# First heads' stacks and negated queries made under the second batch's projections; the opening without 42 unread matmuls

## The reference, cut to what matters

```
x = x + LN(attn(LN(x)))         # 16 heads of 16, rotary q and k, softmax over all 2048 keys, all f32
    q, k = rope(x Wq' + bq), rope(x Wk' + bk);  v = x Wv' + bv
    out  = softmax(q k' / 4) v;  return out Wo' + bo
x = x + LN(ffn(LN(x)))          # 2 layers: windowed attention with 8 heads of 64, then a gated MLP
```

## Time and profile before

| | |
|---|---|
| median of 3 runs | 2952.65 us (2952.53, 2952.65, 2959.49) |
| the profiled execution | 2961.71 us, its span 2959.7 us |
| PE busy in the span | 2797.1 us (95%) |
| DVE, ACT, POOL busy | 2320.3 us, 2116.6 us, 972.5 us |
| mean granted clock of PE | 0.965 of full speed |
| projections / first gap / opening | 0 to 123 us / 123 to 161 us / 147 to 198 us |

### The profile page before, as it was taken

The page is one execution under the profiler, slowest core; times in us unless marked ns, Lnnn a source line. Parts: engine busy times, 40 slices in busy tenths (PEclk is TensorE's granted clock), DMA queues, the critical chain, the costliest instruction groups (busy, mean ns, idle before and its releaser), DMA issues. The chain is left out here.

```text
span 2959.7 us, 59044 instructions
## 1 busy us (share of the span) xinstructions
PE 2797.1 (95%) x22548; PEld 1742.8 (59%) x22548; DVE 2320.3 (78%) x4282; ACT 2116.6 (72%) x4556; POOL 972.5 (33%) x1145
## 2 busy tenths in 40 slices
PE   7689999999999999999976799999999999999997
PEld 7543333333333333333335688888888788888886
DVE  6559999999999999899905577777777677777774
ACT  5458888888888888788854466666666666667664
POOL 6510000010001000000007455555555465665563
PEclk9859999999999999899988799999999999999999
DMA  5612333334343343334212000000000100000000
GB/s 161 173 27 31 59 54 56 53 66 73 61 71 58 62 72 59 57 50 71 41 53 102 3 5 4 5 5 4 5 5 32 54 11 19 19 11 19 19 18 25
DMA packets 84328, 131.32 MB, mean 44 GB/s; under 512 B 32912, under 2 KB 58960, under 8 KB 76240
## 3 DMA queue, kind: packets, MB, share of 16 engines
q1 hardware_dynamic: 77760, 120.41, 20.9%
q10 hardware_dynamic: 6288, 7.14, 0.7%
HBM read 83.98 MB, written 34.60 MB: 40 GB/s over the span
## 5 line engine op out<-in xcount | busy, mean ns | idle before, releaser
L634 ACT ACTIVATE probs<-scores 128x512 f32<-128x512 f32 x2048 | 1114.9, 596 | 203.2 <-PE scores L565 80.8
L667 DVE TENSOR_REDUCE mx<-aux 128x1 f32<-128x1024 f32 x982 | 1201.1, 1223 | 65.7 <-PE aux L533 58.5
L533 PE MATMUL aux<-k_stack,q_stack 48*128 48x512 f32 x2006 | 760.8, 455 | 15.5 <-DVE mx L675 10.5
L565 PE MATMUL scores<-q_stack,k_stack 50*128 50x512 f32 x2048 | 764.6, 452 | 0.0
L578 PE MATMUL pv<-probs,v_ones 128*32 128x256 f32 x8192 | 661.0, 395 | 0.1
L565 PEld LDWEIGHTS scores<-q_stack,k_stack 50*128 50x128 f32 x2048 | 311.1, 186 | 431.1 <-ACT probs L634 413.6
L578 PEld LDWEIGHTS pv<-probs,v_ones 128*32 128x32 f32 x8192 | 161.9, 108 | 362.7 <-ACT probs L634 291.0
L533 PEld LDWEIGHTS aux<-k_stack,q_stack 48*128 48x128 f32 x2006 | 307.9, 189 | 47.0 <-DVE mx L675 21.0
L484 POOL CAST m_parts<-head_max 128x16 fp32r<-128x16 f32 x32 | 6.3, 198 | 933.7 <-DVE head_max L660 933.7
L1399 ACT ACTIVATE VO<-VO,wo_bo_sb 128x256 f32<-128x256 f32 (+1 forms) x512 | 250.9, 491 | 47.3 <-DVE wo_bo_sb L1523 47.0
L1523 DVE CUSTOM_DVE_ANT_0 VO<-bank,mask_sb,wo_bo_sb 128x256 f32<-128x256 f32 (+1 forms) x512 | 216.2, 469 | 56.2 <-PE bank L1229 56.2
(11 more groups left out here) (172 smaller groups left out, 4706.5 us busy)
## 6 DMA issues: line engine op xcount, KB each, us to landing
q_stack<-qk_dram SPq DMA_DIRECT2D x192, 128.0 KB, 5.3
k_stack<-qk_dram SPq DMA_DIRECT2D x192, 128.0 KB, 7.0
qk_dram<-qkT_hi SPq DMA_DIRECT2D x32, 256.0 KB, 3.1
qk_dram<-qkT_lo SPq DMA_DIRECT2D x32, 256.0 KB, 3.6
VO<-o_stage SPq DMA_DIRECT2D x128, 32.0 KB, 7.0
q_minus_first<-sums_dram SPq DMA_DIRECT2D x32, 128.0 KB, 3.0
w_parts<-tables SPq DMA_DIRECT2D x16, 256.0 KB, 2.5
x_in<-x_dram SPq DMA_DIRECT2D x16, 256.0 KB, 3.2
```

Source lines behind the costliest of these rows:

```text
L533: return nc.tensor.matmul(out, q_stack[max_rows, n % BODY, tile * P:(tile + 1) * P], k_stack[max_rows, n % BODY, keys * 512:(keys + 1) * 512],
L565: last = nc.tensor.matmul(out, k_stack[0:SCORE_ROWS, n % BODY, s * P:(s + 1) * P], q_stack[0:SCORE_ROWS, n % BODY, j * 512:(j + 1) * 512], ...
L634: nc.scalar.activation(probs[:, e % PROBS], scores[:, item_of_exp(e) % BANKS1], ACT.Exp, scale=float(D1) ** -0.5).then_inc(act_emptied, 1)
L667: nc.vector.tensor_reduce(mx[:, n % BODY, tile, half:half + 1], aux[:, unit % 2].rearrange("p a k -> p (a k)"), AX.X, ALU.max).then_inc(dv ...
```

## The change

- `q_stack`, `k_stack` and `q_minus_first` belong to a class `Stacks` that is allocated before the projections. The rows of -1 are set by POOL at the beginning of the projection phase.
- In the projection phase SP loads head 0's twelve DMAs behind the stores of group 4 and head 1's twelve behind the stores of group 5. POOL negates in five pieces (4 tiles each of head 0, and 5 of head 1), after its steps 26, 28, 30, 32 and 33.
- SP no longer waits at the end of the projection phase for the stores; it does in the attention phase, before it loads the rows with the maxima of head 0.
- The L593 matmuls (two a tile, 42) are left out.
- Space is made elsewhere: `qk_rot` is written over `qk_cos` (so L143 waits for the transposes of tile `t - 2` instead of for its rotation), the raw weights lie in `VO`, the opening's positive parts in four slots of `probs`, `x1_sb` is a ring of 16 tiles (POOL's L779 waits from the ninth pair on for the store and the reader 16 tiles back), several tiles of the feed-forward phase lie in the stacks, and `b2` is loaded through a DRAM copy.

```diff
+Q_MINUS_PIECES = ((0, 0, 4), (0, 4, 8), (0, 8, 12), (0, 12, TB), (1, 0, LEAD))
@@ project_phase, SP @@
                         sp.dma_start(rows[:, tokens], tile[:, g % 2, c].bitcast(F32)).then_inc(stored[g % 2], 16)
-            for g in range(2):
-                sp.wait_ge(stored[g], 16 * STORES * (NT // GROUP // 2))
+                if g == TB // GROUP:
+                    for parity in range(2):
+                        sp.wait_ge(stored[parity], 16 * STORES * (TB // GROUP // 2))
+                if g in (TB // GROUP, TB // GROUP + 1):
+                    n = g - TB // GROUP
+                    sp.wait_ge(stacks.minus_ones_made, n + 1)
+                    stacks.load(sp, n, 0, stacks.for_scores_loaded)
+                    stacks.load(sp, n, SECOND, stacks.for_max_loaded)
@@ project_phase, DVE @@
-                        dve.wait_ge(rot_done, t - 1)
+                        dve.wait_ge(qkT_in_psum, t - 1)
@@ project_phase, POOL @@
+            for n in range(BODY):
+                nc.gpsimd.memset(stacks.k[SECOND // 2:SECOND, n].bitcast(F32), -1.0).then_inc(stacks.minus_ones_made, 1)
...
+                if t in NEGATED_AT:
+                    negate(NEGATED_AT.index(t))
@@ attention_phase, SP @@
-                if i == 0:
-                    sp.wait_ge(dve_emptied, unit_of[(OPENING - 1) * BLOCKS] + 1)
...
-            load(0, SECOND, for_max_loaded)
-            for n in range(2):
-                sp.wait_ge(minus_ones_made, n + 1)
-                load(n, 0, for_scores_loaded)
-                if n == 0:
-                    load(1, SECOND, for_max_loaded)
+            for parity in range(2):
+                sp.wait_ge(qkT_stored[parity], 16 * STORES * (NT // GROUP // 2))
             load_rows(0)
@@ attention_phase, POOL @@
-            for n in range(BODY):
-                nc.gpsimd.memset(k_stack[SECOND // 2:SECOND, n].bitcast(F32), -1.0).then_inc(minus_ones_made, 1)
-                pool.wait_ge(minus_ones_made, n + 1)
-            for n, start, stop in Q_MINUS_PIECES:
...
             nc.gpsimd.memset(mx[:], LOWEST).then_inc(lowest_made, 1)
@@ attention_phase, PE @@
                 nc.tensor.matmul(out, q_minus_first[rows, t], k_stack[rows, n, k * 512:(k + 1) * 512], start=False, stop=True).then_inc(act_filled, 1)
-                nc.tensor.matmul(pv[:], q_stack[max_rows, n, tile * P:(tile + 1) * P], k_stack[max_rows, n, k * 512:(k + 1) * 512], start=True, stop=True)
@@ attention_phase, ACT @@
+                if e == PROBS - BLOCKS:
+                    act.wait_ge(dve_emptied, unit_of[(OPENING - 1) * BLOCKS] + 1)
@@ output_phase, POOL @@
+                    if 2 * v >= RING:
+                        pool.wait_ge(x1_stored[(2 * v - RING) // 8], 16)
+                        pool.wait_ge(x1_normed, 2 * v + 2 - RING)
```

More of the change, by code:

```diff
@@ L39, with __init__, load, project_phase @@
 QKV_LEAD = 4
-def project_phase(nc, ins, x_sb, VO, qk_dram, ident):
+SPLIT_ROWS = 3 * D1
+SCORE_ROWS = SPLIT_ROWS + 2
+SECOND = P // 2
+BLOCKS = T // 512
+BODY = 3
+VW = 32
+HALF = 256
+STEPS = NH * TB
+LEAD = 5
+OPENING = TB + LEAD
+AHEAD = OPENING * BLOCKS + 1
+FIRST_ROWS = TB + 3
+ROWS_STEP, LARGER_STEP = 13, 11
+PROBS = 3 * BLOCKS
+BANKS1 = 3
+LOADS = 6
+CHUNK = 8
+STORES = 8
+TABLES_HEAD = 27
+LOWEST = -3e38
+Q_MINUS_PIECES = ((0, 0, 4), (0, 4, 8), (0, 8, 12), (0, 12, TB), (1, 0, LEAD))
+class Stacks:
+    def __init__(self, nc, ctx, qk_dram):
+        sb = lambda n, s, d=F32: ctx.enter_context(nc.sbuf_tensor(n, s, d))
+        sem = nc.alloc_semaphore
+        self.qk_dram = qk_dram
+        self.q = sb("q_stack", [P, BODY, T], F32R)
+        self.k = sb("k_stack", [P, BODY, T], F32R)
+        self.q_minus = sb("q_minus_first", [P, OPENING, P], F32R)
+        self.minus_ones_made, self.q_minus_made = sem("minus_ones_made"), sem("q_minus_made")
+        self.for_max_loaded, self.for_scores_loaded = ([sem(f"{name}_loaded{slot}") for slot in range(BODY)] for name in ("for_max", "for_scores"))
+    def load(self, sp, n, row0, loaded):
+        for stack, what, parts in ((self.q, 0, (0, 1, 0)), (self.k, 1, (0, 0, 1))):
+            for i, part in enumerate(parts):
+                sp.dma_start(stack[row0 + i * D1:row0 + (i + 1) * D1, n % BODY, :].bitcast(F32), self.qk_dram[what, part, n]).then_inc(loaded[n % BODY], 16)
+def project_phase(nc, ins, x_sb, VO, qk_dram, ident, stacks, qkT_stored):
     with ExitStack() as ctx:
@@ L66, in project_phase @@
         qk_sin = sb("qk_sin", [P, 2, 2 * C])
-        qk_rot = sb("qk_rot0", [P, 2, 2 * C])
-        hiT = sb("qkT_hi", [P, 2, 4, GROUP * P], F32R)
-        loT = sb("qkT_lo", [P, 2, 4, GROUP * P], F32R)
+        qk_rot = qk_cos
         psT = ps("psT0", [P, 2, 512])
@@ L168, in _, with negate @@
             pool.wait_ge(half_made, 1)
+            for n in range(BODY):
+                nc.gpsimd.memset(stacks.k[SECOND // 2:SECOND, n].bitcast(F32), -1.0).then_inc(stacks.minus_ones_made, 1)
+                pool.wait_ge(stacks.minus_ones_made, n + 1)
+            def negate(i):
+                n, start, stop = Q_MINUS_PIECES[i]
+                rows = slice(0, SPLIT_ROWS)
+                pool.wait_ge(stacks.for_scores_loaded[n], 16 * LOADS)
+                nc.gpsimd.tensor_scalar(stacks.q_minus[rows, n * TB + start:n * TB + stop], stacks.q[rows, n, start * P:stop * P].rearrange("p (t c) -> p t c", c=P).bitcast(F32),
+                                        -1.0, None, ALU.mult).then_inc(stacks.q_minus_made, 1)
+                pool.wait_ge(stacks.q_minus_made, i + 1)
             for t in steps:
@@ L238, in _ @@
                     act.wait_ge(weights_loaded, 16)
-                    nc.scalar.copy(w_hi[:], w_sb[:]).then_inc(w_rounded, 1)
+                    nc.scalar.copy(w_hi[:], w_sb).then_inc(w_rounded, 1)
                     act.wait_ge(bias_loaded, 16)
@@ L371, in _ @@
         def _(sp):
-            def load(n, row0, loaded):
-                for stack, what, parts in ((q_stack, 0, (0, 1, 0)), (k_stack, 1, (0, 0, 1))):
-                    for i, part in enumerate(parts):
-                        sp.dma_start(stack[row0 + i * D1:row0 + (i + 1) * D1, n % BODY, :].bitcast(F32), qk_dram[what, part, n]).then_inc(loaded[n % BODY], 16)
             def load_rows(n):
@@ L752, in _ @@
             load_weights(sp)
-            for start, end in zip(STORES, STORES[1:]):
+            for i, (start, end) in enumerate(zip(STORES2, STORES2[1:])):
                 sp.wait_ge(x1_made, end)
-                sp.dma_start(x1_dram[:, 2 * start:2 * end], x1_sb[:, 2 * start:2 * end]).then_inc(x1_stored, 16)
-            sp.wait_ge(x1_stored, 16 * (len(STORES) - 1))
+                sp.dma_start(x1_dram[:, 2 * start:2 * end], x1_sb[:, 2 * start % RING:2 * (end - 1) % RING + 2]).then_inc(x1_stored[i % 2], 16)
+            for parity, stores in enumerate((3, 2)):
+                sp.wait_ge(x1_stored[parity], 16 * stores)
         @block.gpsimd
@@ L922, in load_w1 @@
         for part in range(2):
[L923 removed]
+            eng.dma_start(self.w1[part].bitcast(F32), self.w1_parts[l, part]).then_inc(self.w1_loaded, 16)
     def load_w2(self, eng, ins, l):
@@ L936, in load_second_wqkv, with feed_forward_phase @@
         eng.dma_start(place[:].bitcast(F32), self.wqkv_parts[part]).then_inc(self.wqkv1_loaded, 16)
-def feed_forward_phase(nc, ins, weights, x_sb, free_space, spare, x1_dram, mask_sb, ident, out):
+def feed_forward_phase(nc, ins, weights, stacks, x_sb, free_space, spare, x1_dram, mask_sb, ident, out):
     with ExitStack() as ctx:
@@ L978, in feed_forward_phase @@
         qks_swapped = sb("qks_swapped", [P, LAYERS, 2, D2])
-        xT_hi, xT_lo = (sb(f"xT3_{part}", [P, 4, NC, P + 1], F32R) for part in ("hi", "lo"))
+        xT_hi, xT_lo = in_k(4, NC, P + 1), in_k(4, NC, P + 1)
         qT = sb("qT3", [P, 4, P])
@@ L1048, in shift @@
                 sp.dma_start(x_mid[1:P, s, 2], x_mid[0:P - 1, s, 1]).then_inc(shifted[v % 2], 16)
-                above = zeros[0:1, :] if first(v) else x_mid[P - 1:P, (v - 2) % 4, 1]
+                above = zeros if first(v) else x_mid[P - 1:P, (v - 2) % 4, 1]
                 if v < 2:
```

125 lines of the change are left out of this document (56 added, 69 removed).

## The result

The changed kernel takes 2940.51 us (median of 20 runs, 2928.62 to 2955.84), the kernel before 2959.25 us beside it on the same chip (20 runs, 2952.37 to 2975.92). The ratio is 0.9933, 95% interval 0.9916 to 0.995: 19.8 us faster, between 14.8 and 24.9. The forecast was 28.4 us faster and 2924.2 us, with 2933 as its upper end. The change works, but gives about two thirds of what was expected.

What follows compares the result with a forecast made beforehand. PE, 95% busy, was taken to bound the kernel, with time to gain where it waits 25.80 and 9.54 us around the opening's start. -28.9 + 0.5 = -28.4 us from 2952.65 gave 2924.2 us, range 2914 to 2933.

Steps and rivals of the forecast that it cites:

- The opening's start and tile 2: Start of attention: PE begins the opening at 128.0, tile 2's first L533 comes at 132.15 instead of 161.05, 28.9 us earlier.
- SP's last issue 0.36 later: End of the projections: POOL's third negation piece delays the last sine products and SP's last stores by 0.36 us, to 127.69.
- the boundary: Between projection and attention blocks: a boundary without a DMA wait costs 0.32 us, so PE starts the opening at 128.0.
- The price of 0 for loads beside stores: Projections: head 0's loads ahead of group 5's stores delay those to 114.9, which costs ACT's path 0 us.
- POOL under the projections: Projection phase: the negation pieces fit into POOL's spare time, priced at 0, at most 0.9 us.
- the start-up fills: Start of the projections: fills of -1 move the first 1/deviation from 5.10 to about 7.7, before ACT's first tile: 0.
- The output phase: Output phase: L779's extra waits in eight pairs, all for things long done, cost between 0 and 16 x 0.06 us, say +0.5.
- The feed-forward phase has the same instructions on other addresses: 0: Feed-forward phase: the same instructions run on other addresses, so its time does not change, 0 us.
- From tile 3 on all is as before: Opening: tile 3 is no later, and from it on everything runs as before, following tile 2's gain of 28.9 us.
- Rival D: Main steps: without unread matmuls the clock stays at 0.50, each us costing 0.45 us; 100 us give 2969; chance 2%.
- The sum: Whole kernel: -28.9 us at the front and +0.5 in the output phase make -28.4 us, 2924.2 us.
- The 42 unread matmuls, direct gain 0: Opening: L593 takes no time of its own beside L590 of the next k, so leaving it out gains 0 directly.

Runs made afterwards that it cites:

- e7: The kernel before with a head's loads for the maxima issued ahead of those for the scores: 2940.19 us, ratio 0.9918.
- e3: The changed kernel with a head's loads for the maxima issued ahead of those for the scores: 2919.01 us, ratio 0.9866.
- e9: The changed kernel with loads for the maxima first and hT 64 bytes further, without the 42 unread matmuls: 2907.77 us, ratio 0.9829.
- e5: The changed kernel with the 42 unread matmuls back, loads for the maxima first and hT 64 bytes further: 2908.78 us, ratio 0.9812.
- e4: The changed kernel with hT, the feed-forward's normalised input, 64 bytes further, at its old offset within 128: 2928.07 us, ratio 0.9893.
- e8: The kernel before with hT moved up 64 bytes to a multiple of 128, as in the changed kernel: 2959.82 us, ratio 0.9992.
- e10: The kernel before with loads for the maxima first and without the 42 unread matmuls: 2942.75 us, ratio 0.9946.
- e2: The kernel before, only without the 42 unread matmuls: 2964.37 us, ratio 1.0034.

## Why the prediction was wrong

*The opening's start and tile 2: right within 1 us.* 27.9 of 28.9 us came. Of the missing 1.0 us, 0.7 is the step "SP's last issue 0.36 later", which measured 128.38 - 127.33 = 1.05, and 0.3 the boundary, 0.59 us instead of 0.32. The delay came by another way than the forecast's: not by POOL's third piece but by group 5's stores, for which ACT waited until 116.55. The price of 0 for loads beside stores was too low by some tenths; the DMAs had no room left (share 0.98).

*POOL under the projections, the start-up fills, `qk_rot` over `qk_cos`: right. The output phase:* forecast at +0.5 us, it went from 66.6 to 65.7.

*"The feed-forward phase has the same instructions on other addresses: 0": this step failed.* The phase got 4.6 us longer (4.4 from e7 to e3). The place of hT alone costs 6 to 8 us (e3 against e9 and e5, e4, and 4 us in e8 the other way); less low clock in the phase, 49 instead of 58 us (50 instead of 56 in e3 and e7), gave 2 to 4 us of it back. I had counted instructions and never asked what an address does to one.

*"From tile 3 on all is as before": this failed too.* The clock came back later after the first main score: 34.6 us and not 17.4 in the profiled run, 23.7 and not 17.3 in e3 and e7. At 0.4 this is 7 and 2.6 us. Most of the rest of the 18.8 us that the profiled run's main steps lost is its stretch of 44 us at low clock against 20 in before, which is chance as far as these runs tell: such stretches fell on either kernel. Why the clock comes back later isn't shown; e5, e7, e9 and e10 leave the 42 unread matmuls little part in it. Rival D named the place and, at 0.45 us for each us, nearly the right price; it was not big enough to decide.

*The sum.* From e7 to e3, without the waits for loads: 29.1 us at the front, less 2.6, 0.2 and 4.4, is 21.9 us, where 28.4 were forecast; the change as made measured 19.8 [14.8, 24.9]. With hT moved it is worth 31 to 35 us.

*The 42 unread matmuls, direct gain 0: right within what e5, e9, e7 and e10 tell.* In the kernels with waits they may be worth more (e2).

*The base.* I subtracted from 2952.65, the median of three runs; over 20 runs the kernel before has 2959.25. This is 6.6 of the 16.3 us between forecast and result, the feed-forward 4 to 5, the later clock 2.6 or more, and the rest is inside the interval. The spread that I took from three runs was 7 us, the true one 24 us (2952.37 to 2975.92), and a part of it has a cause that stood in the trace: PE's waits of up to 0.9 us for loads, and a low clock behind one of them. I had not looked at the main steps, since the change doesn't touch them. The range was too narrow for both reasons.

## What to carry over

When buffers move, the instructions that read them are part of the change: compare the offsets of matmul operands before and after, and allow some us for each hot group (here 3 ns a step on 2112 matmuls, 6 to 8 us). Take the pace from start to start, not from a merged row's length. Where a time has a spread, find its source before forecasting against a median of three; here the order of twelve loads made part of it, and turning it round was worth as much as the change itself (21 us in the changed kernel) and left no low stretch in the middle of the main steps. Issue loads in the order in which they are wanted.
